# Attention gather of a graph layer: a second PSUM place for the spread scores, exponents read from SBUF, the idle products taken out

## The reference

```python
h = jnp.einsum('ni,hio->nho', x, W)                 # 8 heads of 64
s_src = jnp.einsum('nho,ho->nh', h, a_src)
s_tgt = jnp.einsum('nho,ho->nh', h, a_tgt)
e = s_src[src] + s_tgt[tgt]
e = jnp.where(e >= 0, e, NEG_SLOPE * e)
m = jax.ops.segment_max(e, tgt, num_segments=n)
ex = jnp.exp(e - m[tgt])
denom = jax.ops.segment_sum(ex, tgt, num_segments=n)
alpha = ex / (denom[tgt] + 1e-16)
out = jax.ops.segment_sum(h[src] * alpha[:, :, None], tgt, num_segments=n)
```

## Time and profile before

| | us |
|---|---|
| median of 3 runs | 2696.54 |
| lowest and highest | 2694.64, 2700.79 |
| the profiled execution | 2682.08 |
| its span in the trace | 2680.2 |
| TensorE busy | 2209.0 (82%) |
| VectorE busy | 1508.7 (56%) |
| GpSimd busy | 861.7 (32%) |
| ScalarE busy | 692.4 (26%) |
| indirect DMAs of `attend`, line 1928, 372 of them | 352.7 |
| weighing products, line 1973, 93 | 212.1 |
| sum products, line 2086, 1488 | 395.9 |

### The profile page before, as it was taken

How to read it: one execution, slowest core, us unless ns; L and a number is a source line. 1 busy time by engine, 2 the same in 40 slices (tenths; PEclk the granted TensorE clock), 3 DMA queues, 4 the chain that set the end, 5 groups by cost and what they waited for, 6 DMA issues and landing times. The chain is left out here.

```text
span 2680.2 us, 33485 instructions
## 1 busy us (share of the span) xinstructions
PE 2209.0 (82%) x10056; PEld 1407.8 (53%) x10056; DVE 1508.7 (56%) x3023; ACT 692.4 (26%) x1862; POOL 861.7 (32%) x879
## 2 busy tenths in 40 slices
PE   0099997788788887789968938888888888999999
PEld 0055554333343343666645626666666685665665
DVE  6976665567676765533326537777777684121221
ACT  0011111111111111223322234444444333323222
POOL 2000000666666662035541046666666300000000
PEclk9999999799999999679988969999999998999999
DMA  1111111323233235613332157777776630000000
GB/s 46 38 63 63 63 63 73 91 83 85 83 85 90 84 87 45 223 32 60 56 66 75 48 152 198 201 201 201 203 200 201 129 96 1 8 0 9 8 8 8
DMA packets 112805, 236.17 MB, mean 88 GB/s; under 512 B 22584, under 2 KB 67019, under 8 KB 109960
## 3 DMA queue, kind: packets, MB, share of 16 engines
q0 software_dynamic: 56784, 160.68, 23.6%
q1 hardware_dynamic: 55864, 73.57, 8.3%
HBM read 193.62 MB, written 40.57 MB: 87 GB/s over the span
## 5 line engine op out<-in xcount | busy, mean ns | idle before, releaser
L609 POOL DMA_INDIRECT rows<-h_table,row_rel x372 | 358.7, 964 | 649.6 <-SPq L531 440.2
L1928 POOL DMA_INDIRECT rows_g<-g_table,row_src x372 | 352.7, 948 | 347.4 <-POOLq L95 141.8
L2086 PE MATMUL p_ag<-rows_g,oh_g 128*128 128x260 f32 x1488 | 395.9, 400 | 6.9 <-ACT oh_g L2009 5.9
L2086 PEld LDWEIGHTS p_ag<-rows_g,oh_g 128*128 128x128 f32 x1488 | 262.3, 191 | 34.2 <-ACT oh_g L2009 6.0
L864 PE MATMUL p_agg<-rows,oh 128*128 128x256 f32 x744 | 201.7, 406 | 42.2 <-DVE x L660 25.3
L2440 DVE SCALAR_TENSOR_TENSOR x<-p_yf,cw_f,x 128x256 f32<-128x256 f32 (+1 forms) x160 | 66.4, 478 | 281.4 <-PE p_yf L2600 281.4
L1973 DVE TENSOR_TENSOR rows_g<-rows_g,p_e 128x2048 f32<-128x2048 f32 x93 | 212.1, 2281 | 1.9 <-ACT p_e L2030 1.9
L864 PEld LDWEIGHTS p_agg<-rows,oh 128*128 128x128 f32 x744 | 134.6, 194 | 108.8 <-issue 56.6
L729 DVE TENSOR_TENSOR fT<-a_sb,p_sel 128x512 f32<-128x512 f32 x200 | 129.3, 685 | 107.9 <-PE p_sel L912 43.7
L2063 PEld LDWEIGHTS p_n<-node_g,ohT_g 128*128 128x128 bf16 x1116 | 75.3, 97 | 179.9 <-issue 138.9
L2063 PE MATMUL p_n<-node_g,ohT_g 128*128 128x16 bf16 x1116 | 81.4, 170 | 104.9 <-issue 72.2
(11 more groups left out here) (438 smaller groups left out, 3529.0 us busy)
## 6 DMA issues: line engine op xcount, KB each, us to landing
h_table<-h_out SPq DMA_DIRECT2D x20, 1024.0 KB, 3.9
where_g<-d_table SPq DMA_DIRECT2D x93, 128.0 KB
w<-in_L_ffn_W SPq DMA_DIRECT2D x16, 512.0 KB, 8.8
rows<-h_table,row_rel POOLq DMA_INDIRECT x372
rows_g<-g_table,row_src POOLq DMA_INDIRECT x372
g_table<-row SPq DMA_DIRECT2D x20, 260.0 KB
f<-in_L_ffn_W SPq DMA_DIRECT2D x16, 256.0 KB, 5.7
x_acc<-x SPq DMA_DIRECT2D x1, 2560.0 KB
```

What stands on the lines that cost most here:

```text
L609: pool.indirect_dma_start(rows[:, r, j], None, st.h_rows, bass.IndirectOffsetOnAxis(ap=st.row_rel[:, at:at + 1], axis=0)).then_inc(gathere ...
L1928: pool.indirect_dma_start(rows[:, r, j], None, st.g_table, bass.IndirectOffsetOnAxis(ap=st.row_src[:, at:at + 1], axis=0)).then_inc(gather ...
L2086: last = pe.matmul(p_a[:, k % NS, h, 0:HALF], oh[:, r, j], rows[:, r, j, h * HALF:(h + 1) * HALF], start=j % SUP == 0, stop=j % SUP == SUP ...
```

## The change

Three things change in `attend`, and nothing else. `p_n` gets two places, by the batch's parity, and `spread` of batch s waits for the copy of batch s-2 where it waited for that of s-1. `p_e` is gone: the exponential is taken once, into `rows`, without the wait for the previous product, and `weigh` reads its second input from there, in SBUF. The idle products before each round are gone, with the wait for a free place of `p_a` that stood in front of them (the same wait stands before the round's first sum product).

```diff
-        p_n = ps("p_n", [P, 512])
-        p_e = ps("p_e", [P, 512])
+        p_n = ps("p_n", [P, 2, 512])
...
-                ex = p_e[:, 0:BATCH * H].rearrange("p (j h) -> p j h", j=BATCH)
+                ex = rows[:, s % RING, :, HF:]
                 dve.tensor_tensor(feats, feats, ex.unsqueeze(3).broadcast_to([P, BATCH, H, HID1]), ALU.mult).then_inc(msg_ready, 1)
...
-                nc.scalar.copy(n_sb[:, s % 2], p_n[:, 0:EX].rearrange("p (j c) -> p j c", j=BATCH)).then_inc(n_taken, 1)
+                nc.scalar.copy(n_sb[:, s % 2], p_n[:, s % 2, 0:EX].rearrange("p (j c) -> p j c", j=BATCH)).then_inc(n_taken, 1)
...
                 act.wait_ge(score_ready, s + 1)
-                if s:
-                    act.wait_ge(msg_ready, s)
-                nc.scalar.activation(rows[:, s % RING, :, HF:], score[:, s % 2], ACT.Exp)
-                nc.scalar.activation(p_e[:, 0:BATCH * H].rearrange("p (j h) -> p j h", j=BATCH), score[:, s % 2],
-                                     ACT.Exp).then_inc(ex_ready, 1)
+                nc.scalar.activation(rows[:, s % RING, :, HF:], score[:, s % 2], ACT.Exp).then_inc(ex_ready, 1)
...
-                    if s:
-                        pe.wait_ge(n_taken, s)
+                    if s >= 2:
+                        pe.wait_ge(n_taken, s - 1)
                 for k in range(3):
-                    last = pe.matmul(p_n[:, j * NC:(j + 1) * NC], ohT[:, s % NR, j], node[:, s % NR, j // SUP, k],
+                    last = pe.matmul(p_n[:, s % 2, j * NC:(j + 1) * NC], ohT[:, s % NR, j], node[:, s % NR, j // SUP, k],
                                      start=k == 0, stop=k == 2)
...
-                if s > 1:
-                    k = GR * s
-                    pe.wait_ge(agg_added, k - NS + 1)
-                    for h in range(2):
-                        pe.matmul(p_a[:, k % NS, h, HALF:], st.ident[:, :], st.qT[:, 0:512 - HALF], start=True, stop=True,
-                                  skip_group_check=True)
```

## The result

The changed kernel takes 2746.82 us (median of 4 runs, 2736.89 to 2761.31), the kernel before 2698.66 beside it: a ratio of 1.0169, 95% interval 1.0142 to 1.0196, so 48 us slower. The forecast was 2731 us.

A forecast was written before the change was run, and what follows sets the result against it. A loop of waits bounds the kernel at 5.97 us a round, then GpSimd at 6.40: 86 rounds give +37 us, the last batches -2, so 2682 + 35 = 2717, plus 14.5 to the runs' median: 2731 us, range 2692 to 2802.

The forecast's parts named there:

- The hold: In `attend`, a gather starting under the product with two SBUF inputs waits until it ends, losing 0.90 to 2.15 us a round.
- rows 6: Layer-0 gather profile: indirect DMAs starting under a two-SBUF-input one-hot take 1.45 and 1.18 us, under a PSUM-input product 0.95.
- The size of the hold: In `attend`, the held gather loses 1.35 or 1.40 us, making a round 6.4 us; 86 rounds give +37 us.
- The start of the stage: First gathers of `attend`, where ScalarE waited 11.89 us for TensorE's late signal; left as it is in the sum.
- TensorE is not what is late next: In `attend`, TensorE's work falls from 5.97 to 4.2 us a round without idle products (0.93) and the stop (0.83).
- The clock: TensorE in `attend` may drop to 1.2 GHz, up to 8.4 us a round, over 2800 us; taken as nothing, chance 0.05.
- The open cost: In `attend`, TensorE's end-of-round signal is acted on about 2.3 us later, cause not told by the trace.
- the forecast's other loop: In `attend`, one signal from TensorE through copy, scores and product goes around two rounds in 10.8 us, 5.4 us each.
- Rival (1): In `attend`, the late signal stays tied to the gathers: 7.2 us a round, +105 us, 2800 us; chance 0.20.
- Rival (2): In `attend`, the index read isn't blocked: rounds of 5.01 to 5.4 us, 2612 to 2645 us; chance 0.14.
- the 2 us of the last batches: The last two batches of `attend`, past the gathers, lose four idle passes of 1.01 us each: -2 us.
- rival (3): In `attend`, no difference: smallest loss of 0.90 us or TensorE's waiting merely moves; 2689 to 2699 us, chance 0.11.

The follow-up runs named there:

- Experiments 1: Kernel before with only the product's exponents read from SBUF, second exponential and its wait gone: 2660.00 us against 2518.32, ratio 1.0570.
- 2: Changed kernel with its SBUF read undone (exponents taken again into PSUM and read there): 2519.31 us, ratio 1.0001 to the kernel before.
- experiments 3: Kernel before without the idle products and their wait, nothing else: 2519.91 us, ratio 1.0008.
- 4: Kernel before with two places for p_n alone, exponents read from PSUM, idle products kept: 2517.78 us, ratio 0.9998.
- 6: Changed kernel, unchanged, run again on another chip: 2663.10 us, ratio 1.0582 to the kernel before.
- the experiments with the relay: Four kernels with TensorE's signal to the copy sent by way of SyncE and a 4-byte transfer: 2704.33, 2731.96, 2703.21 and 2711.69 us.
- experiments 9: Kernel before with TensorE's signal to the copy sent by way of SyncE and a 4-byte transfer: 2704.33 us, ratio 1.0085.
- 11: Two places for p_n, no idle products, exponents from PSUM, TensorE's signal by SyncE and a 4-byte transfer: 2703.21 us, ratio 1.0085 to the kernel before.
- 12: Kernel before without idle products, TensorE's signal to the copy sent by SyncE and a 4-byte transfer: 2711.69 us, ratio 1.0127.
- the first measurement: Changed kernel against the kernel before, the original comparison: 2746.82 us against 2698.66, ratio 1.0169.
- the third set: Four kernels with TensorE's signal sent through SyncE, on a chip where the kernel before takes 2681.98 us: 2704.33, 2731.96, 2703.21 and 2711.69 us.

## Why the prediction was right

The direction, the place and the mechanism held; the size was 14 us short of the 48, and part of that closeness is luck, as the third point says.

- **The hold.** "Waits, about 0.13 us after its start, until that product ends", with an end 0.82 us after it: 89 held gathers, ends 0.81 to 0.84 us after the product. The two issues of the layer-0 gather were enough to see it. Experiments 1 and 2 show that this part alone makes the whole loss on a chip where the kernel before runs at 5.0 us a round. The rule had an edge that rows 6 couldn't show: a gather that starts within 0.02 us of the product is not held (3 of 92).
- **The size of the hold** is the term that was off. The forecast took 1.35 to 1.40 us a round and 6.40 us in all; measured are 4 x (1.349 - 0.948) = 1.60 and 6.62 us. It placed the product by a fixed distance from the landing of the fourth gather, so that the gather starts 0.75 or 0.80 us into it. In fact the place varies from 0.02 to 1.27 us, 0.54 on average: half the gathers that meet a product start in its first 0.27 us, where the hold costs most. The steady part gained 0.64 us a round where 0.43 was forecast.
- **The start of the stage** was left as it was. Before, ScalarE stood idle 11.89 us until its copy at 1589.61; after, the spread products of batch 1 end at 1572.78 and their copy starts at 1583.95, 11.2 us later. These rows of the start show it, with the first product and the gather that it holds:

```profile
1572.31 0.47 PE L2058 MATMUL p_n<-node_g,ohT_g 128*128 128x16 bf16 x12 [0.81 <-issue]
...
1583.95 0.21 ACT L2022 COPY n_g<-p_n 128x64 f32<-128x64 f32 x1 [9.13 <-remote]
...
1588.16 2.29 DVE L1972 TENSOR_TENSOR rows_g<-rows_g 128x2048 f32<-128x2048 f32 x1 [3.06 <-issue]
1588.47 2.81 POOL L1927 DMA_INDIRECT rows_g<-g_table,row_src  x1 [0.30 <-issue]
```

  Up to the 11th product the stage took 90.1 us before and 83.1 after, 7 less. With 48.3 in the steady part and 6.6 more behind it this makes the 47.9 us. The forecast had 37 for all rounds and 2 less at the end; the 7 us gained at the start, which it did not have, hid a part of what its rounds were short. Nor did the last rounds go as forecast, with the idle products as the only difference: before, with the rows there well in advance, the last three took 4.1, 4.7 and 3.7 us, after, 6.8, 7.0 and 3.7.
- **"TensorE is not what is late next"** held: its idle time before slot 0 didn't set the pace, and experiments 3, 4 and 6 show that its 0.93 us of idle products and the second place are worth nothing against GpSimd. Its busy share, given as about 65%, is 74% in the window of the result, where its clock is lower.
- **The clock** was given 0.05 for costing more. The granted clock fell to 0.89, and cost nothing that can be seen: experiment 1 (0.97) and 6 (0.90) have the same round, 6.61 and 6.64 us. The missing idle products don't lower it by themselves: experiments 2 and 3 have none, and 0.99.
- **The open cost**, the late signal, is absent on two other chips. The forecast used its 2.3 us as a fixed length of the kernel, and with it 5.97 us a round before the change: a loss of 48 us there, and of 145 us where the signal is on time. With the same forecast on that chip (6.40 - 5.01) x 86 the loss would have been put at 120 us. The length isn't fixed either: the experiments with the relay show 0.93 and 2.25 us, always some 1.3 us after the last gather of a round ends. So the 5.4 us of the forecast's other loop, which has the 2.3 in it, had no firm ground. The comparison with GpSimd's rounds didn't turn on it, as those are longer.
- **Rival (1)** was a late signal tied to the gathers, at 7.2 us a round. The tie is there in the kernel before and its like: in the kernel before and in experiments 9, 11 and 12 the signals get through 1.1 to 1.3 us after the end of a round's fourth gather. Its price isn't. In the changed kernel GpSimd hardly ever stops, most copies on the first chip (48 of the 90 from the fourth batch on) follow the spread product by 0.04 us, the others by up to 7 us, and the round is 6.62. **Rival (2)**, no hold, is out.
- **The range** was put together without the 2 us of the last batches that the sum has: its low end is 2692 where rival (3) says 2689. The measured time lies in the middle, so nothing hangs on it.


What makes TensorE's signals late in the first measurement and in the third set stays open; on the chips of the other two sets the same gathers are in flight and the signals are on time. In the changed kernel of the first measurement the late ones (over 0.3 us) are frequent where the spread product ends between two issues (7 of 11) and under a product that holds a gather (16 of 21), and rarer otherwise (12 of 58). All this points to GpSimd's issues, but no run here changes them alone on such a chip, and none tells the cause.

## What to carry to other kernels

Before an input of a long VectorE instruction is moved from PSUM to SBUF, look at what GpSimd issues meanwhile: nearly each indirect DMA that starts under an instruction with two SBUF inputs (89 of 92 here) waits for its end, and with issues 1.25 us apart an instruction of 2.28 us hardly ever misses one. Where the input must be in SBUF, cut the instruction: four pieces brought the loss from 145 us to 23. And a wait that a trace cannot explain may belong to the chip: find out whether it is there on another before its length goes into a sum. In a loop where everything repeats, that the stretches add up to the round proves nothing; what tells loops apart is a run that lengthens one stretch, and which distances stay.

## What the runs showed of the hardware beyond that

- A `tensor_scalar` of 128x2048 f32 with one SBUF input (1.28 us) holds indirect DMAs, too, even one that began 0.34 us before it.
- The same program takes 2518 us on the chips of the first two sets, 2682 us on that of the third and 2699 us in the first measurement. TensorE's signal was acted on after 0.04 us on the former and after 2.3 us in the last; on the chip of the third set SyncE acted on it after 0.9 to 2.3 us (medians), some 1.3 us after the end of a round's last gather in each of three kernels.
- TensorE busy for 299.6 of 300 us (experiment 4) was no bound: with 260 us of work the time was the same.
